# Query groups and value groups placed one by one into the turns of a cross attention loop

## The chip, the cores and the metric

The kernel is one program on one core of one Trainium2 chip. The metric is the device time of one execution in microseconds. Four compute engines work side by side: TensorE (PE in the rows) multiplies matrices into the PSUM banks, VectorE (DVE), ScalarE (ACT) and GpSimd (POOL) work element by element. SyncE (SP) only issues transfers from memory here. Each engine takes its instructions strictly in the order in which the program lists them for it, and they wait for each other by semaphores.

## The reference

The input `x` has 8 sentences of 100 tokens with 512 features, the context 8 x 722 x 512. The model is one block of self attention, cross attention and a feed-forward net, and then a gated feed-forward net. What is computed, cut to the part that matters here (`_ln` is a layer norm; the self attention ahead of it is of the same form):

```python
x = _ln(tgt + sa, g1, be1)
q1 = x @ wq.T + bq
k2 = memory @ wk.T + bk
v2 = memory @ wv.T + bv
cscores = jnp.einsum('btd,bmd->btm', q1, k2) / jnp.sqrt(jnp.float32(DKQ))
ca = jnp.einsum('btm,bmd->btd', jax.nn.softmax(cscores, axis=-1), v2)
x = _ln(x + ca, g2, be2)
ff = jax.nn.relu(x @ w1.T + b1) @ w2.T + b2
return _ln(x + ff, g3, be3)
```

## The kernel before

All products run in split form: each fp32 operand is a high part and a low part (names with H and L), and a product is three matmuls, high by high, high by low and low by high. Writing a split operand takes two steps: ScalarE writes the high part, VectorE subtracts it for the low part.

The work on the 800 tokens is cut in two halves of 400 (4 sentences each) and in *units*, one 512 x 512 weight matrix each. `unit(n, h, groups)` on TensorE multiplies unit n with half h; it has four groups e, one for 128 output features, 12 matmuls of 400 columns each. The function of the same name on ScalarE and VectorE evacuates the groups. `U_A` is the query product: `wq` and `wk` are multiplied with each other in advance, so its result AH, AL meets the raw context. `U_CV` is the value product, behind the attention, because the weights `wv` are applied to the attended context. `U_F` onward are the feed-forward units.

The cross attention goes by sentence b. Its steps on TensorE are:

- `cross_scores(b)`: 24 matmuls, the query columns of sentence b by the transposed context, into banks 4 and 5. For b = 0 and b = 4 it waits for the last group of the query product of that half.
- `cross_prob_transpose(b)`: 6 transposes of the probabilities, into banks 6 and 7. They wait for the exponential of ScalarE (`cross_exp`), which waits for the maximum of VectorE (`cross_max`).
- `cross_attend(b)`: 18 matmuls, probabilities by context, into bank 2.
- `cross_attend_transpose(b)`: 4 transposes of the result, into bank 3.

Beside these, ScalarE and VectorE split each context as it arrives: `split_ct` for the transposed one in two halves, `split_cn` for the plain one in three parts (the low part of the third is GpSimd's). The transfers have one buffer each (`ctR`, `cnR`), and SyncE issues the next one when the split of the last has freed it. `key_bias_rows` and `key_bias_columns` make a term of the scores that depends on the query token; `cross_max(0)` waits for the columns.

The order is written out by hand, once for each engine. Before the loop it has the units `U_A` of both halves, with the first scores between the groups of the second half. In the loop, turn b has `cross_attend(b)`, `cross_prob_transpose(b + 1)`, `cross_scores(b + 2)` and `cross_attend_transpose(b)`; the last two turns have no scores left and take two groups of `U_CV` each. After the loop come `to_tokens`, the second half of `U_CV` and the feed-forward units. GpSimd splits the weights of several units there (`split_weights`, L454), and computes the deviations of the layer norms (L448), for which VectorE's step `nmr` (L1204) waits. The residual input and the weights of the second feed-forward unit are loaded when the transposes of the last turn have been issued (`c_attT`, L408 and after).

The PSUM bank of a group is its number e, but for `(U_CV, 0)`, where it is e % 2, because banks 2 and 3 belong to the loop (`bank`, L301).

Of the kernel before, what the change touches and what calls it, by code (L numbers as in the profile page):

```python
# [110 lines left out]
def build(nc, x, ctxt, ctxn, wvo, wts, consts, g3, be3, out):  # L111
    with ExitStack() as ctx:
# [188 lines left out]
        def bank(n, h, e):  # L301

            return e % 2 if (n, h) == (U_CV, 0) else e

# [202 lines left out]
        def _(pe):  # L507
            def unit(n, h, groups=range(KC)):
                at = POS[n, h]
                mh, ml = operand[n]  # L510
                for e in groups:

                    pn, ph = ORDER[at - 1]
                    if n == U_VO:
                        pe.wait_ge(s_att_low, KC * h + e + 1)
                    elif (n, h) == (U_CV, 0) and e >= 2:
                        pe.wait_ge(dve_evac, dve_count(n, h, e - 2))
                    elif (n, h) == (U_CV, 1):
                        if e < 2:
# [197 lines left out]
            def cross_attend(b):  # L717
                pe.wait_ge(c_probT_low, b + 1)
                if b == 0:
                    pe.wait_ge(dve_evac, dve_count(U_A, 1, 2))  # L720
                else:
                    pe.wait_ge(c_att_sb, b)
# [8 lines left out]
            def cross_attend_transpose(b):  # L731
                pe.wait_ge(c_att_sb, b + 1)
                if b == 0:
                    pe.wait_ge(dve_evac, dve_count(U_A, 1, 3))
                else:
                    pe.wait_ge(c_attT_low, b)
                for k in range(KC):
                    mm = pe.transpose(ps[:, 3, k * T:(k + 1) * T], utok[:, b % 2, k * P:(k + 1) * P],
                                      ident[0:T, 0:T])
                mm.then_inc(c_attT, 1)  # L740
# [56 lines left out]
            key_bias_rows(0)  # L797
            unit(U_A, 1, [0])
            key_bias_rows(1)
            cross_scores(0)  # L800
            unit(U_A, 1, [1])
            key_bias_columns()
            unit(U_A, 1, [2, 3])
            cross_prob_transpose(0)
            cross_scores(1)
            for b in range(B):
                cross_attend(b)
                if b + 1 < B:
                    cross_prob_transpose(b + 1)
                if b + 2 < B:  # L810
                    cross_scores(b + 2)
                else:
                    unit(U_CV, 0, [[0, 1], [2, 3]][b + 2 - B])
                cross_attend_transpose(b)
# [44 lines left out]
        def _(act):  # L859
# [181 lines left out]
            act.wait_ge(gv_ready, 2)  # L1041
            unit(U_A, 1, [0])
            key_bias_rows(0)
            key_bias_rows(1)
            split_ct(1, 0)
            unit(U_A, 1, [1])
            split_ct(1, 1)
            cross_exp(0)
            unit(U_A, 1, [2, 3])
            cross_probT(0)  # L1050
# [3 lines left out]
            for b in range(B):  # L1054
                if b + 1 < B:
                    split_cn(b + 1, 0)
                    split_cn(b + 1, 1)
                cross_attended(b)
                if b + 1 < B:
                    cross_probT(b + 1)  # L1060
                    split_cn(b + 1, 2)
                if b + 3 < B:
                    split_ct(b + 3, 0)
                    split_ct(b + 3, 1)
                if b + 2 >= B:
                    unit(U_CV, 0, [[0, 1], [2, 3]][b + 2 - B])
                if b + 2 < B:
                    cross_exp(b + 2)
                cross_attendedT(b)
                if b == B - 2:  # L1070
# [34 lines left out]
        def _(dve):  # L1105
# [318 lines left out]
            norm_features(1, 1)  # L1424
            unit(U_A, 0)
            unit(U_A, 1, [0])
            split_ct(1, 0)
            unit(U_A, 1, [1])
            dve.wait_ge(c_col, 1)
# [3 lines left out]
            split_ct(1, 1)  # L1433
            unit(U_A, 1, [2, 3])
            cross_recip(0)
# [4 lines left out]
            for b in range(B):  # L1440
                if b + 1 < B:
                    split_cn(b + 1, 0)
                    split_cn(b + 1, 1)
                    cross_recip(b + 1)
                    cross_probT(b + 1)
                if b + 2 < B:
                    cross_max(b + 2)
                if b + 3 < B:
                    split_ct(b + 3, 0)
                if b + 2 >= B:  # L1450
                    unit(U_CV, 0, [[0, 1], [2, 3]][b + 2 - B])
                if b + 3 < B:
# [89 lines left out]
```

## Time and profile before

| | us |
|---|---|
| median of 3 runs (lowest, highest) | 553.06 (553.04, 560.08) |
| the profiled execution | 553.16 |
| its span | 551.4 |
| TensorE busy | 530.0 |
| VectorE, ScalarE, GpSimd busy | 330.0, 221.3, 102.7 |

The span runs from the first to the last instruction; 1.8 us of the profiled execution lie around it. Times in rows count from the start of the span. A matmul's busy time overlaps the next one's, so the distance from start to start is its true price. The number in brackets behind a row is the idle time of the engine just before it and the instruction that ended it.

### The profile page before, as it was taken

What the parts mean: (1) busy time and instruction counts of PE and PEld (TensorE: products, weight loads), DVE (VectorE), ACT (ScalarE), POOL (GpSimd) and SP (SyncE); (2) the same over time, 40 slices, a digit from 0 to 9 for tenths busy, and PEclk for the clock granted to TensorE, in tenths of its full rate; (3) what the DMA queues carried; (4) which work ended last, traced back from release to release, by engine and by line L of the source; (5) the groups of instructions that cost most, each with busy time, mean ns of one, the idle gap of its engine ahead of it and who ended that gap; (6) DMA issues with size and microseconds to landing.
All of it is one profiled execution on the core that took longest, in us unless ns stands there. A gap on an engine that the chain in (4) does not pass through costs nothing.

```text
span 551.4 us, 7561 instructions
## 1 busy us (share of the span) xinstructions
PE 530.0 (96%) x3032; PEld 503.4 (91%) x3032; DVE 330.0 (60%) x551; ACT 221.3 (40%) x387; POOL 102.7 (19%) x95
## 2 busy tenths in 40 slices
PE   7599999999999999998999999998999999999996
PEld 6499999988988788998899999997999999999996
DVE  3783479783588997777675344268494355432225
ACT  2364551455488885165417053304514322220200
POOL 1600151013012225232920000005430000000000
PEclk9799999999999999998999999999999999999999
DMA  8732232020569972532222220102210024010003
GB/s 220 276 147 79 58 126 77 1 107 1 184 217 328 315 240 87 122 112 77 77 77 76 77 77 26 52 0 75 80 76 1 0 77 154 5 73 1 0 1 119
DMA packets 18373, 53.75 MB, mean 97 GB/s; under 512 B 1570, under 2 KB 2370, under 8 KB 15778
## 3 DMA queue, kind: packets, MB, share of 16 engines
q1 hardware_dynamic: 18338, 53.27, 28.9%
q8 instruction: 24, 0.39, 0.3%
q14 instruction: 11, 0.09, 0.0%
HBM read 51.63 MB, written 1.64 MB: 97 GB/s over the span
## 4 chain that ended last, share of the span: by engine, by line
PE 79%; DVE 9%; DMA 6%; issue 2%; ACT 1%; POOL 1%; SPq 1%; DVEq 0%; ACTq 0%
PE ps L538 20%; PE ps L540 20%; PE ps L539 20%; DMA WR<-wts_in 3%; PE ps L582 2%; DMA OR<-wvo_in 2%; PE ps L700 2%; PE ps L702 2%; PE ps L701 2%; PE ps L560 2%; PE ps L728 1%; PE ps L726 1%; PE ps L727 1%; DMA ctR<-ctxt_in 1%; DVE tok L1209 1%
## 5 line engine op out<-in xcount | busy, mean ns | idle before, releaser
L538 PE MATMUL ps<-XH,WH 128*128 128x400 f32 x352 | 122.3, 348 | 1.9 <-DVE XL L1225 1.8
L540 PE MATMUL ps<-XH,WL 128*128 128x400 f32 x352 | 121.5, 345 | 0.0
L539 PE MATMUL ps<-XL,WH 128*128 128x400 f32 x352 | 121.4, 345 | 0.0
L538 PE MATMUL ps<-AH,WH 128*128 128x400 f32 x288 | 101.4, 352 | 4.5 <-DVE AL L1142 4.3
L540 PE MATMUL ps<-AH,WL 128*128 128x400 f32 x288 | 100.5, 349 | 0.0
L539 PE MATMUL ps<-AL,WH 128*128 128x400 f32 x288 | 100.3, 348 | 0.0
L454 POOL TENSOR_TENSOR WL<-WR,WH 128x512 fp32r<-128x512 f32 x40 | 55.1, 1407 | 80.8 <-ACT WH L872 80.8
L538 PEld LDWEIGHTS ps<-XH,WH 128*128 128x128 f32 x352 | 66.1, 188 | 3.4 <-DVE XL L1225 2.4
L539 PEld LDWEIGHTS ps<-XL,WH 128*128 128x128 f32 x352 | 66.1, 188 | 0.0
L540 PEld LDWEIGHTS ps<-XH,WL 128*128 128x128 f32 x352 | 66.2, 188 | 0.0
L538 PEld LDWEIGHTS ps<-AH,WH 128*128 128x128 f32 x288 | 54.9, 191 | 6.5 <-DVE AL L1142 6.1
L1160 DVE TENSOR_TENSOR acc<-ps,acc 128x400 f32<-128x400 f32 x48 | 27.5, 573 | 50.3 <-PE ps L540 49.9
L539 PEld LDWEIGHTS ps<-AL,WH 128*128 128x128 f32 x288 | 54.9, 191 | 0.1
L540 PEld LDWEIGHTS ps<-AH,WL 128*128 128x128 f32 x288 | 54.9, 191 | 0.0
L872 ACT ACTIVATE WH<-WR 128x512 fp32r<-128x512 f32 x84 | 48.4, 626 | 8.2 <-DMA WR<-wts_in 8.1
L904 ACT ACTIVATE AT<-ps,cst 128x400 f32<-128x400 f32 x32 | 19.0, 595 | 79.0 <-PE ps L540 78.9
L908 ACT ACTIVATE AH<-ps 128x400 fp32r<-128x400 f32 x32 | 16.1, 504 | 85.3 <-PE ps L540 85.3
L1145 DVE SCALAR_TENSOR_TENSOR AL<-ps,AH 128x400 fp32r<-128x400 f32 x32 | 18.4, 574 | 42.3 <-ACT AH L908 42.2
L1142 DVE TENSOR_TENSOR AL<-AT,AH 128x400 fp32r<-128x400 f32 x32 | 20.6, 645 | 34.1 <-ACT AH L905 34.0
L1121 DVE TENSOR_TENSOR ctL<-ctR,ctH 128x1444 fp32r<-128x1444 f32 x16 | 26.4, 1659 | 14.7 <-ACT ctH L880 14.6
L1116 DVE TENSOR_TENSOR WL<-WR,WH 128x512 fp32r<-128x512 f32 x44 | 30.2, 711 | 4.5 <-ACT WH L872 4.5
L445 POOL TENSOR_SCALAR veps<-mv 100x4 f32<-100x4 f32 x10 | 4.1, 415 | 143.9 <-DVE mv L1196 143.9
(189 smaller groups left out, 848.7 us busy)
## 6 DMA issues: line engine op xcount, KB each, us to landing
WR<-wts_in SPq DMA_DIRECT2D x20, 1024.0 KB, 4.8
ctR<-ctxt_in SPq DMA_DIRECT2D x16, 722.0 KB, 5.8
cnR<-ctxn_in SPq DMA_DIRECT2D x16, 512.0 KB, 5.9
cnR<-ctxn_in SPq DMA_DIRECT2D x8, 256.0 KB
tok<-x_in SPq DMA_DIRECT2D x4, 400.0 KB
tok<-x_in SPq DMA_DIRECT2D x1, 1600.0 KB
cnR<-ctxn_in SPq DMA_DIRECT2D x8, 160.0 KB
VR<-wvo_in SPq DMA_DIRECT2D x4, 256.0 KB, 7.3
```

What stands on the lines that cost most here:

```text
L454: pool.tensor_tensor(WL[SLOT[n]][:, k, :], WR[:, k, :], raw(WH[SLOT[n]][:, k, :]), ALU.subtract).then_inc(w_low_pool, 1)
L538: pe.matmul(dst, wh, half(mh, h, k), start=(k == 0), stop=False)
L539: pe.matmul(dst, wh, half(ml, h, k), start=False, stop=False)
L540: mm = pe.matmul(dst, wl, half(mh, h, k), start=False, stop=(k == KC - 1))
L872: act.activation(WH[SLOT[n]][:, k, :], WR[:, k, :], ACT.Copy).then_inc(w_high, 1)
L904: act.activation(half(AT, h, e), src, ACT.Relu, bias=cst[:, col:col + 1])
L908: act.activation(half(AH, h, e), src, ACT.Relu).then_inc(act_evac, 1)
L1116: dve.tensor_tensor(WL[SLOT[n]][:, k, :], WR[:, k, :], raw(WH[SLOT[n]][:, k, :]), ALU.subtract).then_inc(w_low, 1)
L1121: dve.tensor_tensor(ctL[b % 2][:, 2 * i:2 * i + 2, 0:M], ctR[:, 2 * i:2 * i + 2, :], raw(ctH[b % 2][:, 2 * i:2 * i + 2, 0:M]), ALU.subtrac ...
L1142: dve.tensor_tensor(half(AL, h, e), half(AT, h, e), raw(half(AH, h, e)), ALU.subtract).then_inc(dve_evac, 1)
L1145: dve.scalar_tensor_tensor(out=half(AL, h, e), in0=src, scalar=0.0, in1=raw(half(AH, h, e)), op0=ALU.max, op1=ALU.subtract).then_inc(dve_e ...
L1160: dve.tensor_tensor(half(acc, h, e), src, half(acc, h, e), ALU.add).then_inc(dve_evac, 1)
```

## The change

The diff moves calls. No instruction is added or taken away.

- Of the query product's second half, `(U_A, 1)`, group 0 now follows `cross_scores(0)`, and groups 1, 2 and 3 go into turns 0, 1 and 2, between `cross_attend(b)` and `cross_prob_transpose(b + 1)`.
- Of the value product's first half, `(U_CV, 0)`, groups 0 to 3 go into turns 4 to 7, ahead of `cross_attend_transpose(b)`.
- `(U_A, 1)` uses banks 0 and 1 in turn, as `(U_CV, 0)` does, with the waits that follow from it.
- ScalarE and VectorE have their evacuations at the matching places. On both, the second half of context 1 (`split_ct(1, 1)`) now stands behind `cross_exp(0)` and `cross_max(0)`; on ScalarE it stood ahead.

```diff
--- before.py
+++ after.py
@@ -300,7 +300,7 @@
 
         def bank(n, h, e):
 
-            return e % 2 if (n, h) == (U_CV, 0) else e
+            return e % 2 if (n, h) in ((U_A, 1), (U_CV, 0)) else e
 
         def raw(ap):
             return ap.bitcast(F32)
@@ -513,8 +513,10 @@
                     pn, ph = ORDER[at - 1]
                     if n == U_VO:
                         pe.wait_ge(s_att_low, KC * h + e + 1)
-                    elif (n, h) == (U_CV, 0) and e >= 2:
+                    elif (n, h) in ((U_A, 1), (U_CV, 0)) and e >= 2:
                         pe.wait_ge(dve_evac, dve_count(n, h, e - 2))
+                    elif (n, h) == (U_CV, 0):
+                        pe.wait_ge(dve_evac, dve_count(U_A, 1, e + 2))
                     elif (n, h) == (U_CV, 1):
                         if e < 2:
                             pe.wait_ge(dve_evac, dve_count(U_CV, 0, e + 2))
@@ -717,7 +719,7 @@
             def cross_attend(b):
                 pe.wait_ge(c_probT_low, b + 1)
                 if b == 0:
-                    pe.wait_ge(dve_evac, dve_count(U_A, 1, 2))
+                    pe.wait_ge(dve_evac, dve_count(U_A, 0, 2))
                 else:
                     pe.wait_ge(c_att_sb, b)
                 for c in range(MC):
@@ -731,7 +733,7 @@
             def cross_attend_transpose(b):
                 pe.wait_ge(c_att_sb, b + 1)
                 if b == 0:
-                    pe.wait_ge(dve_evac, dve_count(U_A, 1, 3))
+                    pe.wait_ge(dve_evac, dve_count(U_A, 0, 3))
                 else:
                     pe.wait_ge(c_attT_low, b)
                 for k in range(KC):
@@ -795,22 +797,22 @@
             to_features(1, 1, tiles[1])
             unit(U_A, 0)
             key_bias_rows(0)
-            unit(U_A, 1, [0])
             key_bias_rows(1)
             cross_scores(0)
-            unit(U_A, 1, [1])
+            unit(U_A, 1, [0])
             key_bias_columns()
-            unit(U_A, 1, [2, 3])
             cross_prob_transpose(0)
             cross_scores(1)
             for b in range(B):
                 cross_attend(b)
+                if b < KC - 1:
+                    unit(U_A, 1, [b + 1])
                 if b + 1 < B:
                     cross_prob_transpose(b + 1)
                 if b + 2 < B:
                     cross_scores(b + 2)
-                else:
-                    unit(U_CV, 0, [[0, 1], [2, 3]][b + 2 - B])
+                if b >= HB:
+                    unit(U_CV, 0, [b - HB])
                 cross_attend_transpose(b)
             to_tokens(2, 0, U_CV, XS)
             unit(U_CV, 1, [0, 1, 2])
@@ -1039,14 +1041,12 @@
             norm_features(1, 1)
             unit(U_A, 0)
             act.wait_ge(gv_ready, 2)
-            unit(U_A, 1, [0])
             key_bias_rows(0)
             key_bias_rows(1)
             split_ct(1, 0)
-            unit(U_A, 1, [1])
+            unit(U_A, 1, [0])
+            cross_exp(0)
             split_ct(1, 1)
-            cross_exp(0)
-            unit(U_A, 1, [2, 3])
             cross_probT(0)
             split_ct(2, 0)
             cross_exp(1)
@@ -1056,16 +1056,18 @@
                     split_cn(b + 1, 0)
                     split_cn(b + 1, 1)
                 cross_attended(b)
+                if b < KC - 1:
+                    unit(U_A, 1, [b + 1])
                 if b + 1 < B:
                     cross_probT(b + 1)
                     split_cn(b + 1, 2)
                 if b + 3 < B:
                     split_ct(b + 3, 0)
                     split_ct(b + 3, 1)
-                if b + 2 >= B:
-                    unit(U_CV, 0, [[0, 1], [2, 3]][b + 2 - B])
                 if b + 2 < B:
                     cross_exp(b + 2)
+                if b >= HB:
+                    unit(U_CV, 0, [b - HB])
                 cross_attendedT(b)
                 if b == B - 2:
                     for k in range(KC):
@@ -1423,15 +1425,13 @@
             affine_features(1, 1)
             norm_features(1, 1)
             unit(U_A, 0)
+            split_ct(1, 0)
             unit(U_A, 1, [0])
-            split_ct(1, 0)
-            unit(U_A, 1, [1])
             dve.wait_ge(c_col, 1)
             dve.tensor_copy(cshift[:, :], ps[0:T, 6, 0:B]).then_inc(c_col_sb, 1)
             dve.wait_ge(c_col_sb, 1)
             cross_max(0)
             split_ct(1, 1)
-            unit(U_A, 1, [2, 3])
             cross_recip(0)
             cross_probT(0)
             split_ct(2, 0)
@@ -1441,14 +1441,17 @@
                 if b + 1 < B:
                     split_cn(b + 1, 0)
                     split_cn(b + 1, 1)
+                if b < KC - 1:
+                    unit(U_A, 1, [b + 1])
+                if b + 1 < B:
                     cross_recip(b + 1)
                     cross_probT(b + 1)
                 if b + 2 < B:
                     cross_max(b + 2)
                 if b + 3 < B:
                     split_ct(b + 3, 0)
-                if b + 2 >= B:
-                    unit(U_CV, 0, [[0, 1], [2, 3]][b + 2 - B])
+                if b >= HB:
+                    unit(U_CV, 0, [b - HB])
                 if b + 3 < B:
                     split_ct(b + 3, 1)
                 cross_attendedT(b)
```

How the rows move at three places. In the changed kernel TensorE's lines have numbers that are 2 higher. The first place is TensorE behind the last matmuls ahead of the key bias columns (`crow`), before:

```order
L540 MATMUL ps<-XH_50,WL_105 128x400
L681 MATMUL ps<-ones_129,crow 100x1 [waits c_row_sb]
L681 MATMUL ps<-ones_129,crow 100x1 x7
L538 MATMUL ps<-XH_50,WH_101 128x400 [waits dve_evac]
L539 MATMUL ps<-XL_52,WH_101 128x400
L540 MATMUL ps<-XH_50,WL_105 128x400
```

And after the change:

```order
L542 MATMUL ps<-XH_50,WL_105 128x400
L683 MATMUL ps<-ones_129,crow 100x1 [waits c_row_sb]
L683 MATMUL ps<-ones_129,crow 100x1 x7
L715 MATMUL ps<-ident,prob_82 128x100 [waits c_col_sb,pads_set,c_exp]
L715 MATMUL ps<-ident,prob_82 128x100 x5
L702 MATMUL ps<-ctH_77,AH_63 100x362 [waits ct_low,pads_set,c_exp]
```

Before, two query groups (24 matmuls) stand between the columns and the transposes of `prob`; now the transposes follow the columns directly.

The second place is ScalarE there, from the evacuation of query group 0 of the second half or the key bias rows on, before:

```order
L901 ACTIVATE AH_64<-ps,gv 128x400 [waits gemm_done,gv_ready]
L961 ACTIVATE crow<-ps,qk_125 2x400 [waits c_row] x2
L880 ACTIVATE ctH_77<-ctR 128x2x722 [waits to_feat,ct_loaded0]
L901 ACTIVATE AH_64<-ps,gv 128x400 [waits gemm_done]
L880 ACTIVATE ctH_77<-ctR 128x2x722 [waits to_feat,ct_loaded1]
L968 ACTIVATE prob_82,ssum<-ps,snb 100x722 [waits c_max]
L901 ACTIVATE AH_64<-ps,gv 128x400 [waits gemm_done] x2
L976 ACTIVATE ptH_84<-ps 128x600 [waits c_probT]
```

And after the change:

```order
L963 ACTIVATE crow<-ps,qk_125 2x400 [waits c_row,gv_ready]
L963 ACTIVATE crow<-ps,qk_125 2x400 [waits c_row]
L882 ACTIVATE ctH_77<-ctR 128x2x722 [waits to_feat,ct_loaded0]
L903 ACTIVATE AH_64<-ps,gv 128x400 [waits gemm_done]
L970 ACTIVATE prob_82,ssum<-ps,snb 100x722 [waits c_max]
L882 ACTIVATE ctH_77<-ctR 128x2x722 [waits to_feat,ct_loaded1]
L978 ACTIVATE ptH_84<-ps 128x600 [waits c_probT]
L882 ACTIVATE ctH_76<-ctR 128x2x722 [waits c_scores,ct_loaded0]
```

The exponential (`prob`) has moved ahead of the second split of `ctH_77`, and the evacuations of the later groups (`AH_64`) are gone from here.

The third place is TensorE in turn 2, around the scores of sentence 4 (those with `AH_64`), before:

```order
L727 MATMUL ps<-cnL,ptH_84 100x512
L728 MATMUL ps<-cnH,ptL_86 100x512
L713 MATMUL ps<-ident,prob_83 128x100 [waits c_probT_low,pads_set,c_exp]
L713 MATMUL ps<-ident,prob_83 128x100 x5
L700 MATMUL ps<-ctH_76,AH_64 100x362 [waits pads_set,ct_low,c_exp,dve_evac]
L701 MATMUL ps<-ctL_78,AH_64 100x362
```

And after the change:

```order
L540 MATMUL ps<-XH_50,WH_101 128x400
L541 MATMUL ps<-XL_52,WH_101 128x400
L542 MATMUL ps<-XH_50,WL_105 128x400
L715 MATMUL ps<-ident,prob_83 128x100 [waits c_probT_low,pads_set,c_exp]
L715 MATMUL ps<-ident,prob_83 128x100 x5
L702 MATMUL ps<-ctH_76,AH_64 100x362 [waits pads_set,ct_low,c_exp,dve_evac]
L703 MATMUL ps<-ctL_78,AH_64 100x362
```

The scores of sentence 4 waited for a query group that had been evacuated before the loop; now that group's matmuls (`XH_50`) are just ahead of the transposes.

## Rows read from the trace of the kernel before

**Rows 1.** The page: busy time over the span, and the granted clock in 40 slices.

```profile
span 551.4 us, 7561 instructions
...
PE 530.0 (96%) x3032; PEld 503.4 (91%) x3032; DVE 330.0 (60%) x551; ACT 221.3 (40%) x387; POOL 102.7 (19%) x95
...
PEclk9799999999999999998999999999999999999999
```

**Rows 2.** Windows of two turns: length, busy by engine (count), clock, DMA share, GB/s.

```profile
155.46:164.48 9.02, 9.02 (x53) 7.72 (x52) 8.67 (x10) 8.44 (x11) 2.41 (x1) 1.00 0.66 229
...
192.11:201.73 9.62, 9.25 (x53) 7.65 (x53) 8.80 (x11) 8.03 (x11) 2.40 (x1) 1.00 0.94 317
...
sum 55.36, PE 54.88 PEld 46.04 DVE 49.95 ACT 46.00 POOL 14.41; mean PE 9.15 PEld 7.67 DVE 8.33 ACT 7.67 POOL 2.40
```

**Rows 3.** Timeline of TensorE: start, busy, engine, line, operation, count [idle before].

```profile
140.85 1.57 PE L681 MATMUL ps<-ones,crow 2*100 2x1 f32 x16
...
142.35 0.45 PE L538 MATMUL ps<-XH,WH 128*128 128x400 f32 x1
...
146.84 0.68 PE L713 MATMUL ps<-ident,prob 100*128 100x100 f32 x6
...
147.30 0.39 PE L700 MATMUL ps<-ctH,AH 128*100 128x362 f32 x1
...
151.33 0.39 PE L726 MATMUL ps<-cnH,ptH 128*100 128x512 f32 x1
...
201.73 0.73 PE L713 MATMUL ps<-ident,prob 100*128 100x100 f32 x6 [0.37 <-ACT prob L968]
```

**Rows 4.** Timeline of VectorE, the head of the cross attention.

```profile
142.46 0.17 DVE L1430 COPY cshift<-ps 100x8 f32<-100x8 f32 x1 [0.24 <-PE ps L681]
...
143.93 1.66 DVE L1121 TENSOR_TENSOR ctL<-ctR,ctH 128x1444 fp32r<-128x1444 f32 x1
...
147.67 0.63 DVE L1138 SCALAR_TENSOR_TENSOR AL<-ps,gv,AH 128x400 fp32r<-128x400 f32 x1 [1.52 <-ACT AH L901]
```

**Rows 5.** Timeline of ScalarE, the head of the cross attention.

```profile
141.45 1.40 ACT L880 ACTIVATE ctH<-ctR 128x1444 fp32r<-128x1444 f32 x1
...
144.81 0.19 ACT L968 ACTIVATION_READ_ACCUMULATOR prob<-ps,snb 100x1 f32 x1
...
147.04 0.59 ACT L901 ACTIVATE AH<-ps,gv 128x400 fp32r<-128x400 f32 x1 [1.55 <-PE ps L540]
...
147.56 0.67 ACT L976 ACTIVATE ptH<-ps 128x600 fp32r<-128x600 f32 x1
```

**Rows 6.** Windows of 2 us behind a long and a short idle time of TensorE.

```profile
252.00:254.00 2.00, 2.00 (x7) 1.87 (x8) 0.27 (x1) 0.00 (x0) 0.00 (x0) 0.50 0.95 397
...
266.00:268.00 2.00, 2.00 (x13) 2.00 (x12) 1.56 (x2) 1.08 (x2) 2.00 (x2) 1.00 0.34 70
```

**Rows 7.** Timeline of TensorE around idle times behind the loop.

```profile
233.35 1.54 PE L560 MATMUL ps<-ident,xn 100*128 100x100 f32 x16
...
251.84 0.68 PE L538 MATMUL ps<-AH,WH 128*128 128x400 f32 x1 [2.06 <-DVE AL L1142]
...
253.99 2.18 PE L560 MATMUL ps<-ident,xn 100*128 100x100 f32 x16
...
265.42 0.45 PE L538 MATMUL ps<-XH,WH 128*128 128x400 f32 x1 [1.01 <-DVE XL L1225]
...
384.60 0.45 PE L538 MATMUL ps<-AH,WH 128*128 128x400 f32 x1 [1.25 <-DVE AL L1142]
```

**Rows 8.** Timelines of VectorE and GpSimd where they meet behind the loop.

```profile
214.59 2.21 DVE L1154 TENSOR_TENSOR XS<-XS,XL 128x400 f32<-128x400 f32 x1
...
247.37 2.50 DVE L1204 SCALAR_TENSOR_TENSOR nmr<-mv,rstd 100x4 f32<-100x4 f32 x1 [1.24 <-POOL rstd L448]
...
213.98 2.40 POOL L459 TENSOR_TENSOR cnL<-cnR,cnH 128x1024 fp32r<-128x1024 f32 x1 [5.45 <-ACT cnH L887]
...
247.31 2.54 POOL L454 TENSOR_TENSOR WL<-WR,WH 128x512 fp32r<-128x512 f32 x2
```

## The prediction

> **What bounds the kernel now.** I read the page first [rows 1]: TensorE is busy for nearly the whole span and its granted clock is at full speed but in a few slices. A move of work between stages can then change only three things: time in which TensorE stands still, time in which its clock is down, and the length of the last stage. The diff adds and removes no instruction, so the question is where TensorE waits before and after.
>
> Next the windows of the cross attention loop, cut at the first matmul of each probability transpose [rows 2]. One turn without a wait is 9.02 us (18 value matmuls, 6 transposes, 24 score matmuls, 4 transposes). The six turns there take 55.36 us where six times 9.02 is 54.12: the loop loses 1.24 us in all. In the turns that lose, VectorE is busy for 8.8 us and the DMA share is 0.94: the loop sits close to three limits at once. The timeline shows how the loss looks: at 201.73 the transposes wait 0.37 us for ScalarE's exponential [rows 3], which stands in ScalarE's queue behind the split of a context half that was late from memory. So 1.2 us is all that the loop can give back.
>
> Then the head of the loop, in the timelines of TensorE, VectorE and ScalarE [rows 3 to 5]. The key bias columns start at 140.85, and the transposes of sentence 0's probabilities at 146.84, without a wait. Between them lie two query groups, 142.35 to 146.84, 24 matmuls, 2.2 us a group. Behind this cover runs a chain: the columns, the shift copy on VectorE (142.46), the maximum and two small steps there, and on ScalarE the exponential, whose sum is read out by 145.00 (144.81 and 0.19).
>
> **The change, term by term.**
>
> (a) *The head of the loop loses its cover.* In the changed order the probability transposes stand directly behind the columns. The columns start earlier (the scores and one group are ahead of them, two groups no longer are), but the chain behind them keeps its length: VectorE starts 1.61 us after the first column matmul (142.46 less 140.85), the exponential and its read-out end at 145.00, and 0.05 us goes for the semaphore: 4.20 us from the first column. TensorE's own work there is 1.50 us (140.85 to 142.35). It stands for 4.20 - 1.50 = 2.7 us. Nothing else shortens the chain: the evacuation of the group ahead of the columns (0.59 us on ScalarE, 0.63 us on VectorE, rows of the same form in [rows 4, 5]) ends before the columns do. Bounds: 2.5 to 2.9 us. **+2.7 us.**
>
> (b) *What follows the stall.* Two effects overlap here. First, ScalarE now takes the second half of context 1 behind the exponential, where before it took it ahead (141.45). Counted from the transposes: the copy starts 0.05 us earlier, takes 1.40 us, then come 1.66 us on VectorE [rows 4, 5] and a semaphore, so the half is ready at about +3.05 us. TensorE wants it after 6 transposes (0.46 us, 146.84 to 147.30) and 12 of the 24 score matmuls (half of 147.30 to 151.33, 2.0 us), at +2.46 us. That is a wait of 0.6 us. Second, the clock. After an idle time of 2.06 us before 251.84 the granted clock is 0.50 of full speed (1.2 instead of 2.4 GHz) in 252 to 254, six matmuls take 2.15 us instead of 1.1 (0.187 us each, as 24 of them in 4.49 us at the head), and 16 transposes 2.18 us instead of the 1.54 us that the same form has at 233.35 [rows 6, 7]: about 1.7 us lost. After 1.01 us at 265.42 the clock stays at 1.00. An idle time of 2.7 us is nearest to the first of these, so I take a fall, which costs 1.7 us less what the transposes at its start hide of their latency, 1.5 us. The slow score matmuls arrive later than the split half, so the 0.6 us wait is swallowed. Bounds: 0.5 us (no fall) to 2.3 us (a fall and the wait in full). **+1.5 us.**
>
> (c) *Scores of sentence 4.* They need the last query group of half 1, and that group now stands just ahead of transposes 3 and scores 4 in turn 2. The same group before: its matmuls end at 146.84, ScalarE writes AH at 147.04, VectorE AL from 147.67 to 148.30 [rows 3 to 5]. So the group is ready 1.5 us after its end, and TensorE has 0.46 us of transposes to do in that time: it waits 1.0 us. Before, this evacuation lay beside scores 1. Queued ahead of it on VectorE are two context splits, whose last input is a copy begun after the fourth chunk of the value product, well over 3 us earlier; they don't delay it. Behind it wait the reciprocal and the probability split of the next turn, which have a whole score block to spare. Bounds: 0.8 us to 1.0 and a clock fall of 1.7 on top, since at 384.60 a wait of 1.25 us, with others just ahead of it, was followed by one. As the single gap of 1.01 us is nearer, no fall. **+1.0 us.**
>
> (d) *The loop's own waits.* Turns 0 to 2 and 4 to 7 get one group each, 2.2 us of TensorE against 0.6 us more on VectorE (AL) or 1.2 us (the two residual steps), so turns of 9.1 to 9.6 us become 11.2 us. The context loads are issued as splits free the buffers, one set per turn, so they get the same time. Turn 3 stays at 9.0 us, with the slack gathered in front of it. I take all of the 1.24 us back. Bounds: 0.6 to 1.24. **-1.2 us.**
>
> (e) *The end of the loop.* In turn 6 the cover of transposes 7's evacuation shrinks from two groups to one, 2.2 us, plus 0.46 and 0.3 us of transposes. Behind the transposes ScalarE needs 0.67 us (147.56) and VectorE less than 1 us (600 columns, between 0.63 us for 400 and 1.66 us for 1444), some 1.9 us with semaphores [rows 4, 5]. Priced at nothing; if the splits are late again, up to 0.5 us. The order of the last turn from the last value group on is the same as before, and the residual load starts off the same transposes. GpSimd's weight splits for the feed-forward do slide by about 3 us against TensorE, onto the last XS step. Row: the XS step at 214.59 took 2.21 us while GpSimd's split, 213.98, ran for 2.40 [rows 8]; such a step can cost TensorE 0.3 us here, but it falls ahead of a wait of 2.06 us at 251.84 that hangs on loads issued at the loop's end, which takes it in. **0.** The GPSIMD Engine Reference of the Trainium skill, Specifications table, says that GpSimd's SBUF interfaces are shared with VectorE and contend with VectorE instructions that have two SBUF inputs; by that rule the XS step would always wait, and the sum would be the same because of that later wait. The trace agrees in the row above.
>
> **Sum:** 2.7 + 1.5 + 1.0 - 1.2 = +4.0 us. The profiled execution took 553.16 us (span 551.4 us), so **the forecast is 557.2 us**; the median of the runs, 553.06 us, is 0.1 us below that execution.
>
> **Rivals.**
>
> *Clock stays up in (b).* Only the 0.6 us wait is paid: 556.2 us. For it speaks that at 265.42 a wait was forgiven; against it that 2.7 us is longer than every gap here that was forgiven. Chance 0.12.
>
> *The clock also falls in (c).* +1.7 us: 558.9 us. For it: 384.60. Chance 0.15.
>
> *The loop stays bound by loads and VectorE.* Turn 3 and its neighbours keep half of their loss, and turn 6 waits for its probabilities: +0.6 and +0.5 us, 558.3 us. Against it: the turns around are 2 us longer than the DMA share of 0.94 needs. Chance 0.10.
>
> *Not slower: the collision at 247 comes undone.* VectorE's tiny step nmr started at 247.37 and took 2.50 us, because GpSimd had begun a 128x512 weight split at 247.31 [rows 8]; the wait of 2.06 us and the slow clock behind it follow from this. If that step gets ahead of GpSimd by the 0.06 us that it lacked, both go, 2.06 + 1.7 = 3.8 us: 553.4 us. It decides on whether the split's input from ScalarE is later than the statistics; that was ready well before, and both sides hang on the same end of the loop as before, so the chance is 0.05.
>
> *Not slower by interleaving alone.* Perfetto Trace Analysis of the Trainium skill, Optimization Strategy, says that performance may be improved by interleaving regimes whose most contended engine differs, which is what this change does with matmul-bound groups and the loop. As a mechanism of this kernel: the groups widen the turns, (d) is earned, and (a) to (c) must be hidden, 551.9 us. It would need over 2.5 us of other TensorE work behind the columns, and the order has none. Chance 0.03.
>
> That leaves 0.55 for the forecast.
>
> **Numbers.** Lowest of the likely sums: 2.5 + 0.5 + 0.8 - 1.24 = +2.6, 555.6 us. Highest: 2.9 + 2.3 + 1.0 + 1.7 - 0.6 = +7.3, 560.5 us, which needs all at once. A range of 555.0 to 559.4 us holds the forecast, the first three rivals, and leaves out the two that are not slower and the corner. A measurement of this kernel can tell about 2%, 11 us, from no change. Within 2%: 0.97. Slower by over 2%: 0.02, all upper bounds and a lasting clock fall. Faster by over 2%: 0.01, since it would take away half of the 21.4 us in which TensorE is not busy [rows 1].
>
> **What would show it.** For (a): the transposes behind the key bias columns with about 2.6 us of idle time released by the exponential. For (b): the granted clock at half in the 3 us behind that, and score matmuls 0.3 us apart. For (c): one idle time of 1.0 us at a score matmul of turn 2, released by AL. For (d): turns of 11.2 us and one of 9.0, with no wait at the transposes. For (e): an unchanged wait of about 2 us some 27 us after the last turn. The forecast is wrong if something fills the gap behind the columns, or if the waits after the loop move.

## The result, and the profile after

| | before | with the change |
|---|---|---|
| median of 20 runs, us (lowest to highest) | 555.0 (549.38 to 560.08) | 557.98 (554.45 to 562.09) |
| the profiled execution, its span, us | 553.16, 551.4 | 555.6, 553.8 |

The ratio is 1.0062, with a 95% interval of 1.0038 to 1.0086: the change makes the kernel 3.4 us slower (2.1 to 4.8). It leaves out executions in a slower state, over 1.5% above the fastest of the same kernel, so it is not that of the two medians, which lie 3.0 us apart. The forecast was +4.0 us.

One execution differs from the next by several us, so from here on stages are measured within traces. The distance that serves for this is the one from the first matmul of the key bias rows (129.42 us in the first trace of before, 129.45 with the change) to the transposes of the last turn (224.62 and 228.34). I call it the stretch: **95.20 us before and 98.89 us with the change, 3.69 us more**.

TensorE's timeline of the changed kernel, at the head of the loop, at the scores of sentence 4 and behind the loop (columns as in [rows 3]):

```profile
138.67 1.57 PE L683 MATMUL ps<-ones,crow 2*100 2x1 f32 x16
...
142.87 1.26 PE L715 MATMUL ps<-ident,prob 100*128 100x100 f32 x6 [2.63 <-ACT prob L970]
143.83 0.60 PE L702 MATMUL ps<-ctH,AH 128*100 128x362 f32 x1
...
146.04 0.37 PE L703 MATMUL ps<-ctL,AH 128*100 128x362 f32 x1
...
148.88 0.39 PE L728 MATMUL ps<-cnH,ptH 128*100 128x512 f32 x1
...
177.50 0.68 PE L715 MATMUL ps<-ident,prob 100*128 100x100 f32 x6
...
179.02 0.41 PE L702 MATMUL ps<-ctH,AH 128*100 128x362 f32 x1 [0.84 <-DVE AL L1140]
...
256.38 0.45 PE L540 MATMUL ps<-AH,WH 128*128 128x400 f32 x1 [2.90 <-DVE AL L1144]
257.59 1.54 PE L562 MATMUL ps<-ident,xn 100*128 100x100 f32 x16
```

The transposes start 4.20 us after the columns, which is what the chain needed in [rows 3 to 5], and TensorE now stands for 2.63 us ahead of them, until the exponential is there. From 142.87 to 148.88 the 6 transposes and 24 score matmuls take 6.01 us; the same work took 4.49 us in [rows 3], 146.84 to 151.33. The clock shows why, in windows of the changed kernel (columns as in [rows 2]):

```profile
144.00:146.00 2.00, 2.00 (x8) 1.90 (x8) 1.86 (x3) 1.94 (x3) 0.00 (x0) 0.50 0.00 0
146.00:148.00 2.00, 2.00 (x13) 1.97 (x13) 2.00 (x2) 0.13 (x1) 0.00 (x0) 0.97 0.44 110
```

Half clock for 144 to 146, where the scores start about 0.30 us apart, and back at full speed with the matmul at 146.04. And the turns of the loop, cut as in [rows 2]:

```profile
155.19:166.36 11.17, 11.17 (x65) 9.91 (x64) 9.20 (x13) 8.65 (x12) 2.42 (x1) 1.00 0.81 266
166.36:177.50 11.14, 11.14 (x65) 9.90 (x64) 8.54 (x12) 8.56 (x11) 2.41 (x1) 1.00 0.80 265
177.50:187.59 10.09, 9.25 (x53) 7.79 (x52) 6.41 (x9) 7.62 (x10) 2.41 (x1) 1.00 0.67 226
187.59:196.55 8.96, 8.96 (x53) 7.71 (x52) 7.92 (x11) 7.06 (x10) 2.72 (x1) 1.00 0.99 324
196.55:207.74 11.19, 11.19 (x65) 9.91 (x64) 10.17 (x15) 9.49 (x12) 2.40 (x1) 1.00 0.77 267
207.74:218.93 11.19, 11.19 (x65) 9.92 (x64) 7.19 (x12) 5.78 (x8) 2.40 (x1) 1.00 0.42 134
```

These six windows are called turns 1 to 6 from here on: turn k runs from the transposes of sentence k to those of sentence k + 1. The scores of sentence 4, which the program lists in its turn 2 behind the transposes, fall into the third window. Every turn with a group takes 11.2 us and a turn without one 8.96 us; the only loss left is in the third window, at those scores.

### The profile page after: what moved, and what is told of

It is laid out like the page before. It is cut to its first block, busy times and chain, and to the rows that moved or that the text cites. A ratio compares the mean times of both kernels' runs of the same rounds, so it can differ in the third digit from the quotient of the medians.

```text
span 553.8 us, 7561 instructions
## 1 busy us (share of the span) xinstructions
PE 529.2 (96%) x3032; PEld 503.5 (91%) x3032; DVE 326.9 (59%) x551; ACT 222.4 (40%) x387; POOL 102.8 (19%) x95
## 4 chain that ended last, share of the span: by engine, by line
PE 82%; DVE 8%; DMA 5%; ACT 1%; issue 1%; POOL 1%; SPq 1%; DVEq 0%; ACTq 0%
PE ps L540 20%; PE ps L542 20%; PE ps L541 20%; DMA WR<-wts_in 3%; PE ps L702 2%; PE ps L728 2%; PE ps L729 2%; PE ps L730 2%; PE ps L704 2%; PE ps L703 2%; PE ps L584 2%; DMA OR<-wvo_in 2%; PE ps L562 2%; DVE tok L1211 1%; PE ps L595 1%
## 5 line engine op out<-in xcount | busy, mean ns | idle before, releaser
L459 POOL TENSOR_TENSOR cnL<-cnR,cnH 128x1024 fp32r<-128x1024 f32 x7 | 17.2, 2452 | 75.6 <-ACT cnH L889 75.6
```

Of the source, the lines that this page charges most:

```text
L459: pool.tensor_tensor(cnL[:, 2 * i:2 * i + 2, :], cnR[:, 2 * i:2 * i + 2, :], raw(cnH[:, 2 * i:2 * i + 2, :]), ALU.subtract).then_inc(cn_lo ...
```

## The experiments

Eleven runs follow: eight new kernels, and second traces of three. Where only the stretch matters, there is one trace of a kernel.

**The columns first.** The changed kernel, with the chain given its cover back:

```diff
+            key_bias_columns()
             unit(U_A, 1, [0])
-            key_bias_columns()
             cross_prob_transpose(0)
```

with the evacuations and `split_ct(1, 1)` placed to match on ScalarE and VectorE.

> The changed kernel, with the key bias columns ahead of query group 0 of the second half instead of behind it, on all engines, and with the second half of context 1 split ahead of the exponential. Mark: start of the transposes of the last turn, 224.62 us before, 228.34 with the change. My theory (the chain behind the columns lost its cover): the group, 2.2 us, covers the chain again, the idle time at the first probability transposes falls from 2.63 to about 0.5 us, the clock stays up there, the mark comes 2.2 + 1.5 = 3.7 us earlier, at 224.6 to 224.8, with the 0.84 us idle time at the scores of sentence 4 left. Rival (the loop with wider turns is what costs): the mark stays at 228 us though the idle time at the head is gone.

```profile
137.83 1.57 PE L683 MATMUL ps<-ones,crow 2*100 2x1 f32 x16
142.03 0.73 PE L715 MATMUL ps<-ident,prob 100*128 100x100 f32 x6 [0.24 <-ACT prob L970]
```

TensorE's timeline again: the distance from the columns to the transposes is still 4.20 us, but 2.2 us of it is now a query group, and the idle time is 0.24 us. The cross attention begins 4.54 us behind the transposes, at full clock. The absolute mark is 226.03 us because everything ahead of the key bias rows came 1.4 us late in this execution (they start at 130.82). The stretch is 95.21 us, 3.68 us less than with the change, to 0.02 us the expected 3.7: 2.21 us of it ahead of the transposes, where one group covers that much of (a)'s 2.7, and 1.47 us behind them, which is (b). The rival, that the wide turns cost, falls.

**A filler in the gap.** The changed kernel with matmuls that nobody needs:

```diff
             key_bias_columns()
+            for _ in range(14):
+                pe.matmul(ps[:, 3, 0:HALF], WH[SLOT[U_A]][:, 0, 0:P], half(XH, 1, 0), start=True, stop=True)
             cross_prob_transpose(0)
```

> The changed kernel, with 14 further matmuls of the 400-column form behind the key bias columns, whose result in bank 3 nobody reads. They take about 2.6 us, which is the time that TensorE stands there, so they add no work to the path. My theory (b) has two parts, the clock and a late split of context 1: with the clock kept up, the score matmuls run at 0.17 us from start to start, and only the wait for the split, 0.6 us, is left: cross attend of sentence 0 begins at 147.9 instead of 148.88, the mark at 227.4. Rival (the clock falls for another reason than the standing time): half speed in 143 to 146 us as before, mark at 228.3 or later.

Windows and timeline of TensorE in this kernel:

```profile
142.00:144.00 2.00, 2.00 (x16) 1.83 (x15) 0.05 (x1) 1.92 (x3) 0.00 (x0) 1.00 0.00 0
144.00:146.00 2.00, 1.81 (x11) 1.49 (x9) 1.63 (x2) 2.00 (x3) 0.00 (x0) 1.00 0.00 0
```

```profile
138.89 1.57 PE L683 MATMUL ps<-ones,crow 2*100 2x1 f32 x16
140.39 2.87 PE L805 MATMUL ps<-XH,WH 128*128 128x400 f32 x14
143.09 0.73 PE L715 MATMUL ps<-ident,prob 100*128 100x100 f32 x6
...
146.09 0.41 PE L702 MATMUL ps<-ctH,AH 128*100 128x362 f32 x1 [0.27 <-DVE ctL L1125]
...
148.14 0.39 PE L728 MATMUL ps<-cnH,ptH 128*100 128x512 f32 x1
```

The transposes start no earlier (4.20 us again), the clock stays at 1.00, and now the wait for the split half shows, at 146.09. From the transposes to the cross attention it is 5.05 us, against 6.01 with the change and 4.49 before. So with the clock up 0.56 us of (b)'s 1.52 us is left, the late split, which the slow clock had hidden; the other 0.96 us is the clock. Stretch 97.95 us, 0.94 us less than with the change.

**The last query group early.** The changed kernel with

```diff
-                if b < KC - 1:
-                    unit(U_A, 1, [b + 1])
+                if b < 2:
+                    unit(U_A, 1, [[1, 2], [3]][b])
```

on all three engines.

> The changed kernel, with query groups 1 and 2 both in turn 0 and group 3 in turn 1, so that turn 2 has none. My theory (c): the idle time at the scores of sentence 4 (0.84 us, and 1.06 us from start to start) goes, turn 2 takes 9.0 us, the mark comes 1.0 us earlier, at 227.3. Rival (turn 2 without its group is short of time for loads and splits and waits for its exponential, as turns before the change did): the same 0.3 to 1 us comes back as idle time at probability transposes of turns 2 to 4, mark at 227.7 to 228.3.

Windows of turns 2 and 3:

```profile
169.65:178.61 8.96, 8.96 (x53) 7.72 (x52) 6.36 (x9) 7.61 (x10) 2.40 (x1) 1.00 0.80 253
178.61:187.61 9.00, 9.00 (x53) 7.73 (x52) 7.95 (x11) 7.45 (x10) 2.72 (x1) 1.00 0.90 316
```

The idle time at sentence 4 is gone, turn 1 takes 11.17 us, and no turn waits for its exponential. The stretch is 98.02 us, 0.87 us less than with the change. Of what is missing to the 1.06 us of (c), 0.08 us is the way from the transposes of sentence 0 to the cross attention, 6.09 us here instead of 6.01; the other 0.1 us lies in turns 3 to 5, 9.00, 9.03 and 11.25 us. (c) stands as forecast, and the rival falls: the idle time of 0.3 to 1 us that it named did not come back.

**Only the value groups moved**: the kernel before with the `U_CV` part of the diff alone, on all three engines, here TensorE's:

```diff
-                    unit(U_CV, 0, [[0, 1], [2, 3]][b + 2 - B])
...
+                    unit(U_CV, 0, [b - HB])
```

> The kernel before, with only the value product's groups placed one by one into turns 4 to 7; the query groups stay ahead of the loop. My theory (d): of the 1.24 us that the loop lost, only the part in turn 5, whose transposes came 0.60 us late, is won back, since turn 4 gets 2.2 us more; turns 1 to 4 keep their 0.07 to 0.3 us. Mark at 224.0 us (224.62 before). Rival (the order of the value groups is worth as much as the whole 1.24 us): mark at 223.4. Rival (fewer matmuls in turn 6 uncover the evacuation of the last probabilities): an idle time there and a mark at 224.6 or later.

It came out on neither side: the mark was late, as in the second rival, but not by an idle time in turn 6. Turns 5 and 6 were as expected, 11.19 us each, but turns 2 and 3 lost 0.9 and 1.2 us, and the stretch was 96.12 us, 0.9 more than in the first trace of before. ScalarE's timeline in turn 2 shows what was late:

```profile
166.71 1.06 ACT L887 ACTIVATE cnH<-cnR 128x1024 fp32r<-128x1024 f32 x1 [1.95 <-DMA cnR<-ctxn_in]
```

A transfer: ScalarE stood for 1.95 us until it had landed. The expectation had missed that the loop before may lose a different amount in each execution. The next three traces are about that.

**The kernel before again:**

> The kernel before, unchanged, for a second trace of it. In the values-only trial turns 2 and 3 lost 0.9 and 1.2 us because the third context's plain part landed late, which the first trace of before does not show. Theory (the loop before has no slack against the transfers, so that its loss differs from one execution to the next): turns 1 to 6 lose another amount than 1.24 us here, anything from 0.5 to 3 us, and the loss stands where ScalarE or VectorE waited for ctR or cnR. Rival (the loss of the values-only trial came from its order): turns as in the first trace, within 0.1 us each. The waits behind the loop (2.06, 1.01, 0.86, 1.25 us) stay within 0.2 us, the places where the clock falls may differ.

Windows of turns 4 to 6, TensorE's row at the loss, and ScalarE's row ahead of it:

```profile
183.94:193.36 9.42, 9.22 (x53) 7.64 (x53) 8.85 (x11) 8.04 (x11) 2.41 (x1) 1.00 0.97 329
193.36:204.19 10.83, 9.24 (x52) 7.65 (x52) 8.89 (x11) 8.03 (x11) 2.40 (x1) 1.00 0.89 284
204.19:213.28 9.09, 9.09 (x52) 7.80 (x53) 6.95 (x10) 6.56 (x11) 2.40 (x1) 1.00 0.50 151
```

```profile
204.19 0.74 PE L713 MATMUL ps<-ident,prob 100*128 100x100 f32 x6 [1.59 <-ACT prob L968]
```

```profile
200.16 1.41 ACT L880 ACTIVATE ctH<-ctR 128x1444 fp32r<-128x1444 f32 x1 [2.48 <-DMA ctR<-ctxt_in]
```

The loss stands in turn 5, as in [rows 2] and [rows 3], by the same chain, but with 1.59 us of idle time instead of 0.37. The stretch is 96.37 us. With the nmr-first kernel below, whose loop is that of before, there are three: 95.20, 96.37, 96.05.

**The values-only kernel again:**

> The values-only kernel for a second trace; in the first its turns 2 and 3 lost 0.9 and 1.2 us. Theory (the loss there came from late transfers of that execution, not from its order): turns 1 to 4 lose another amount, turns 5 and 6 are 11.2 us again with no loss; distance between 94.5 and 96.2. Rival (its order delays the transfers of turns 2 and 3): the same two turns lose 0.8 us or more each again.

Its six turns took 9.02, 9.04, 9.24, 10.05, 11.27 and 11.19 us, the stretch 95.22 us. Turns 2 and 3, which had lost 2.2 us, lost 0.2 us, so that loss was the execution's; what remains stands in the window before the first turn with a value group (10.05), where before has it one turn later as well. What the value groups' part alone is worth can't be told from two traces (96.12 and 95.22 us) against the three with before's loop.

**The change again:**

> The changed kernel, unchanged, for a second trace. Theory: distance from the key bias rows to the last transposes 98.9 us within 0.2 (turns of 11.2 and 9.0 have no waits that transfers could lengthen), while the kernel before has had 95.2 to 96.4. Idle time at the first probability transposes 2.63 us, with half clock behind it. Behind the loop the clock may fall at other waits than in the first trace. Rival (its first trace was lucky in the loop): distance over 99.5.

Turns of 11.17, 11.15, 10.09, 8.95, 11.19 and 11.19 us: the loop repeats to 0.02 us, and so do the waits of 2.63 and 0.83 us. The stretch was 99.64 us, not within the 0.2 that I gave, and the 0.75 us is all between the transposes of sentence 0 and of sentence 1. 12 score matmuls ran slow instead of 7:

```profile
142.00:144.00 2.00, 0.00 (x0) 0.00 (x0) 1.05 (x3) 0.84 (x2) 0.00 (x0) 0.53 0.00 0
144.00:146.00 2.00, 1.84 (x9) 1.81 (x10) 0.56 (x1) 1.95 (x4) 0.00 (x0) 0.50 0.00 0
146.00:148.00 2.00, 2.00 (x9) 1.88 (x8) 2.00 (x4) 1.43 (x2) 0.00 (x0) 0.50 0.00 0
```

The same idle time, another cost: here the clock was still down in 146 to 148. The rival of 99.5 us and more was met in the number, but not by the loop.

**One group back behind the columns.** From the changed kernel, with groups 2 and 3 in turns 0 and 1 of the program, and on ScalarE `split_ct(1, 1)` ahead of the exponential again (here TensorE's part):

```diff
             unit(U_A, 1, [0])
             key_bias_columns()
+            unit(U_A, 1, [1])
             cross_prob_transpose(0)
...
-                if b < KC - 1:
-                    unit(U_A, 1, [b + 1])
+                if b < 2:
+                    unit(U_A, 1, [b + 2])
```

> The changed kernel with one query group, number 1, back behind the key bias columns, groups 2 and 3 in turns 0 and 1, and the second half of context 1 split ahead of the exponential. Distance from the first key bias row matmul to the transposes of the last turn: 95.2 us before, 98.89 with the change, 95.21 with the columns first. My theory (a), (b) and (c) together: idle time at the first probability transposes about 0.5 us, none at the scores of sentence 4, turns of 11.2 and 9.0 us, distance 94.1 us. Time 1.1 us less than before, ratio 0.998; against the change's ratio of 1.0062. Rival (turns 2 and 3 without a group lose time to the transfers again): distance 94.5 to 95.5, ratio 0.999 to 1.001.

Stretch 94.39 us, 4.50 less than with the change, between the 94.1 expected and the rival's 94.5. Ratio to before 0.9993 (0.9965 to 1.0021), 12 runs: it can't be told from before any more, and the interval holds both the expected 0.998 and the rival's range.

**nmr first**, in the kernel before:

```diff
             split_weights(U_F + 1, [0, 1])
             inverse_deviation(5, 1)
+            pool.wait_ge(nmr_ready, 4)
             split_weights(U_F + 1, [2, 3])
```

> The kernel before, with GpSimd waiting for VectorE's step nmr of the second half ahead of the third chunk of its weight split behind the loop. Theory (the wait of 2.06 us and nmr's 2.50 us are one collision of VectorE and GpSimd): nmr takes 0.16 us, xn starts 2.3 us earlier, the wait falls to 0.5 to 1.1 us (the last AL steps still meet the split), and where the clock fell behind it, it stays up: 1 to 3 us less, ratio 0.995 to 0.998. Rival (the wait hangs on the weights' landing, not on the collision): the wait stays at 2 us and the time is the same.

VectorE's, GpSimd's and TensorE's timelines in this kernel, against [rows 8]:

```profile
250.07 0.16 DVE L1205 SCALAR_TENSOR_TENSOR nmr<-mv,rstd 100x4 f32<-100x4 f32 x1 [1.24 <-POOL rstd L448]
250.15 1.52 DVE L1210 TENSOR_SCALAR xn<-ps,mv,rstd 100x512 f32<-100x512 f32 x2
```

```profile
250.31 2.98 POOL L454 TENSOR_TENSOR WL<-WR,WH 128x512 fp32r<-128x512 f32 x2 [0.28 <-DVE nmr L1205]
```

```profile
253.78 0.45 PE L539 MATMUL ps<-AH,WH 128*128 128x400 f32 x1 [0.75 <-DVE AL L1143]
```

The step takes 0.16 us instead of 2.50, TensorE's wait there is 0.75 us instead of 2.06, and no clock fall follows in this trace. Ratio 0.9963 (0.9945 to 0.9981), 10 runs: 2.0 us faster than before.

**Both edits**, group back and nmr first, and **both with the columns first** as well. The last one's edit against the changed kernel, beside the `pool.wait_ge` and with ScalarE and VectorE to match (here TensorE's part):

```diff
-            unit(U_A, 1, [0])
             key_bias_columns()
+            unit(U_A, 1, [0, 1])
             cross_prob_transpose(0)
...
-                if b < KC - 1:
-                    unit(U_A, 1, [b + 1])
+                if b < 2:
+                    unit(U_A, 1, [b + 2])
```

> The group-back kernel and the nmr-first edit together. If both act by themselves, the time is 2 to 4 us less than before, ratio 0.993 to 0.996. Rival (an earlier gain is taken back by the wait behind the loop, which hangs on transfers issued at the loop's end): it is no better than the better of the two.

> The kernel with both edits, and the key bias columns ahead of query group 0 as well, so that groups 0 and 1 stand behind the columns and 2 and 3 in turns 0 and 1. Theory: the exponential's chain, 2.7 us behind the columns' own work, is covered by 4.4 us of matmuls, the last 0.4 us of standing time at the first probability transposes goes, distance from the key bias rows to the last transposes 94.0 us at most (94.39 and 94.13 in the two group-back kernels), ratio 0.992 to 0.995. Rival (the head was already free, what is left is transfers): the same as the kernel with both edits, 0.994.

| | stretch, us | ratio to before (interval) |
|---|---|---|
| group back | 94.39 | 0.9993 (0.9965 to 1.0021) |
| both | 94.13 | 0.9940 (0.9915 to 0.9965) |
| both, columns first | 93.68 | 0.9918 (0.9885 to 0.9951) |

```profile
138.06 1.57 PE L684 MATMUL ps<-ones,crow 2*100 2x1 f32 x16
144.03 0.68 PE L716 MATMUL ps<-ident,prob 100*128 100x100 f32 x6
148.52 0.39 PE L729 MATMUL ps<-cnH,ptH 128*100 128x512 f32 x1
```

```profile
154.83:166.01 11.18, 11.18 (x66) 9.91 (x64) 9.20 (x13) 8.58 (x12) 2.40 (x1) 1.00 0.80 268
166.01:174.97 8.96, 8.96 (x53) 7.72 (x52) 6.36 (x9) 7.72 (x10) 2.40 (x1) 1.00 0.77 252
174.97:183.97 9.00, 9.00 (x54) 7.73 (x53) 7.95 (x11) 7.46 (x10) 2.72 (x1) 1.00 0.94 321
183.97:192.93 8.96, 8.96 (x54) 7.71 (x53) 7.66 (x11) 7.02 (x9) 2.39 (x1) 1.00 0.94 313
```

The last kernel, in TensorE's timeline and windows: no idle time at the transposes, the cross attention 4.49 us behind them as before the change, and no turn that loses. It is the fastest of these kernels: a median of 549.12 us against 553.91, by the ratio 4.5 us less (2.7 to 6.4), a little more than the expected 0.992 to 0.995 gave. Whether the last edit adds to the one before can't be told by the intervals, which overlap; by the stretch, one trace each, it adds 0.45 us. For the same reason the whole time does not show that the group back adds to nmr first: 0.9940 (0.9915 to 0.9965) against 0.9963 (0.9945 to 0.9981).

## Why the prediction was right, point by point

The time was inside the range, and the forecast 0.6 us above what the runs showed. So close a hit in the whole time is in part luck: the traces of before's loop and of the change, taken in pairs, put the difference of their stretches anywhere from 2.5 us (98.89 less 96.37) to 4.4 us (99.64 less 95.20). By its steps:

- **(a), +2.7.** Right. It is 4.20 us from columns to transposes in all the kernels where the chain is bare or half covered, with an idle time of 2.63 us, which fell to 0.24 and 0.23 us when a group came back.
- **(b), +1.5.** Right in the sum: 1.52 us. Right in its parts too: a wait for the split of 0.56 us (0.6 forecast) lay under the slow clock, as the filler showed. But its size is not fixed; the second trace had 2.2 us (6.72 us from the transposes to the cross attention), near the upper bound of 2.3. The reason given for the fall, that 2.7 us is longer than every idle time that was forgiven, was weaker than it looked: the fall came in all three traces with the 2.63 us, but behind the loop 2.90 us brought none.
- **(c), +1.0.** Right: 1.06 us from start to start (177.50 to 179.02 is 1.52 us, against the 0.46 us of [rows 3]), 0.84 us of it as idle time, released by AL, and no clock fall.
- **(d), -1.2.** Right that all of the loop's own loss is won back. Its size was a little low even in the first trace, since a turn without a wait takes 8.96 us and not the 9.02 us from which it was counted: six times 8.96 is 53.76, so the loss was 1.6 us, and 2.7 + 1.5 + 1.1 - 1.6 gives the stretch's 3.7 us. The size was also read from one trace: the three traces with before's loop have stretches of 95.20 to 96.37 us, so the loss, counted from 9.02 us, was 1.2 us at the least and 2.4 us in the worst. A high DMA share is not what decides: turn 4 of the change had 0.99 in the first trace and 0.97 in the second, more than the 0.94 of before's slow turn, and took 8.96 and 8.95 us without a wait. With the mean of the three, 95.87 us, the change's stretch is 3.0 us longer in its first trace and 3.8 us in its second. The ratio's 3.4 us lies between.
- **(e), 0.** The last turn was as forecast and cost nothing. GpSimd's collision fell on an earlier XS step (the third value group's, VectorE L1156 at 222.53, 1.72 us), beside a context split and not a weight split, and no wait of TensorE followed from it. The part that did not hold is "unchanged", and a move of this wait was one of the prediction's own signs of being wrong: it was 2.90 us instead of 2.06, where the weights landed 16.6 us after their issue instead of 15.8, and 2.37 us in the second trace (16.1 us). Whether the change does this is not shown: the filler kernel and the columns-first kernel, whose loops end in the same way, waited 2.06 and 2.02 us. By luck no clock fall followed in the first trace, which gave 1.6 us back, so that at the first transposes of the feed-forward's result (363.29 and 366.27) the change was only 2.98 us behind.

Of the rivals, the clock fall at (c) and the loop that stays bound did not come. The collision at nmr stayed (251.94, 2.47 us), as given a chance of 0.05 to come undone; its price, 3.8 us, was too high as a mean. Undone on purpose it brought 2.0 us (1.1 to 3.0), since a wait of 0.75 us is left there, and the clock does not fall at that place in every execution. What the Trainium skill says in Perfetto Trace Analysis, Optimization Strategy, that interleaving stages with different limits may pay, held by the stretch: with the head covered, 94.39 and 93.68 us against 95.20 to 96.37. It says nothing of the chain that the moved groups were hiding, and that chain was the larger number here.

Two of the recorded sums count from the median of 553.06 us and the others from 553.16: on the latter base the rival in which the clock stays up gives 556.3 us and the lowest sum 555.7 us, 0.1 us more each. Neither moves the range.

## What to carry to other kernels

Before work is moved away from a place, measure from start to start what runs behind it on the other engines: matmuls without any idle time ahead of them can be the cover of a chain. Here 4.49 us of them hid 2.7 us of one. The change put three query groups into the loop; with only two of them there, and one or two left behind the columns, the stretch was shorter than before (94.39 and 93.68 us against 95.20 to 96.37). In the whole time that gain does not show by itself (0.9993). Price a loop that is close to its transfers from more than one trace, since its loss is what differs between executions, and read stages from a mark inside the trace when the whole time moves by more than the effect.

## What the runs showed of the hardware

- **How long TensorE stands does not decide alone whether its clock falls.** At the same place behind the loop the clock fell after idle times of 2.06, 2.00, 2.18, 2.06 and 2.37 us (before twice, group back, filler, the change's second trace), and did not after 2.90, 2.02 and 2.33 us (the change's first trace, both values-only traces). The stretch from there to the first transposes of the feed-forward's result tells them apart: 111.45 to 111.51 us with the fall, 109.85 to 109.89 without, so it costs 1.6 us. In the four traces in which the waits at this place were 0.30 to 0.89 us none has a fall there, and there is none after the 1.59 us in turn 5 of before's second trace; yet at 384.60 in [rows 7] one came after 1.25 us, with other waits just ahead. The columns-first trace fits neither value: its stretch from there is 115.05 us, with a fall after 2.02 us at this place and another after 2.10 us at 267.92, about 3.2 us over the lower value. The other 2 us are two longer waits: 2.10 us where the other traces have 1.01 to 1.03, and 1.09 us at 279.54 where they have 0.16 or 0.17.
- **The slow time need not begin with the first matmul.** In the change's second trace the clock was at 0.53 in a window in which TensorE issued nothing, and still at 0.50 in 146 to 148.
- **A tiny VectorE step can be held for two GpSimd instructions in a row.** nmr, 100x4 elements, took 0.16 us ahead of GpSimd's weight splits. Begun 0.06 us behind the first of them, it took 2.50 us, as long as the two splits together (2.54 us); in the trace with the last query group early it took 1.25 us, as long as one of them, and TensorE's wait was 0.40 us.
- **Transfers of equal size and order make ScalarE wait differently** from one execution of a kernel to the next: 1.95 us for cnR in turn 2 of one trace of the values-only kernel and 0.25 us in the other, 0.82 and 2.48 us for ctR in turn 5 of the two traces of before. Before's loop passes that on to TensorE; the turns that a group has widened do not.
